# Full 128-column weights for the low halves of the probabilities, and scores issued last in a step, in an image attention kernel

## The chip, the cores and the metric

The kernel runs on one core of one Trainium2 chip. The metric is the time of one execution on the device in microseconds (us), lower is better. The core has a matrix engine (TensorE, PE in the profile, its weight loads PEld), a vector engine (VectorE, DVE), an activation engine (ScalarE, ACT), a third elementwise engine (GpSimd, POOL), and SyncE (SP), which starts most transfers. Each engine runs its own list of instructions in order; they wait for one another by semaphores alone.

## The reference

For each of 8 images x of 128 channels and 32 x 32 = 1024 positions:

```
g = x . w_g + b_g            (1024 x 64)
theta = x . w_theta + b_theta (1024 x 64);  phi = w_phi . x + b_phi (64 x 1024)
att = softmax(theta . phi)    (1024 x 1024, over the last axis)
y   = att . g                 (1024 x 64)
out = x + batch_norm(y . w_out + b_out)
```

The batch norm has fixed mean and variance, so it is a scale and a shift for each channel. All in fp32.

## The kernel before

**Tiles and steps.** An image has MT = 8 tiles of 128 query rows, so there are 64 tiles. Everything is a software pipeline over tiles: in step k, PE works on tile k+1 (scores), tile k-2 (transposes) and the values of an earlier group. Below, "step j" is step k with j = k % 8, the position in an image. A part of four tiles is a half image (512 queries).

**One tile's way.** PE multiplies theta and phi into a tile of scores, 128 x 1024, in PSUM (line 601, four matmuls of 512 columns: a product of high and low parts). DVE takes the row maximum (496), ACT the exponential with its row sum (455), DVE the reciprocal of the sum (518), POOL scales the probabilities by it (316), PE transposes them in eight pieces of 128 x 128 (663), ACT writes the fp16 high half pt_hi (446) and DVE the fp16 low half pt_lo (566), each in two instructions of 512 columns.

**Values.** `weighted_sum` sums y over the eight groups of 128 keys. g is split into two fp16 parts that lie beside each other in the 128 weight columns: columns 0 to 63 high, 64 to 127 low. In each step one quarter (two groups of keys) of a half image is added, to all 512 queries: two matmuls of the high halves with all 128 columns (616), two of the low halves with the 64 high columns alone (620). Of these two, one writes PSUM partitions 0 to 63 and the other 64 to 127, so they use the two column halves of the array ("column tiles"). The output weights stand twice one above the other, so the convolution (628) adds both halves of the partitions.

**Extras.** The next image is prepared in the same steps through one PSUM bank, ps_misc: its projections in steps 0 and 1 (687, three matmuls each), the output convolution of a finished half in steps 2 and 6 (628), g in step 3 (702), its transposition in step 4 (709), and the spread of g's largest value over the partitions after the values of step 7 (607). As all of them use ps_misc, each waits until its last user has been read: the projection of step 0 waits for g_peak_read, which DVE gives after reading the spread maximum in its own step 0 (535), and g in step 3 waits for result_ready, which DVE gives after adding the convolution to the residual in its own step 3 (501). Both waits stand for images 1 to 6; image 0 has neither, and image 7, having no next image, has no such extras.

**Order on DVE.** DVE's step k is written as: reciprocal of tile k-1, residual (j = 3, 7), largest value of g (j = 6) or its reading (j = 0), pt_lo of tile k-2 (twice), and last the row maximum of tile k+1. So the row maximum of tile k+1 stands in front of everything of step k+1.

**Order on ACT and POOL.** ACT's step k: extras, pt_hi of tile k-2 twice, exponential of tile k. POOL's step k: scaling of tile k-1, then extras. The images are run by a loop of two images for each turn, with steps before and after it written out.

Of the kernel before, what the change touches and what calls it, by code (L numbers as in the profile page):

```python
# [23 lines left out]
def build_nonlocal_attention(nc, x, w_tp_t, w_g_t, w_out_t, channel_vectors, out):  # L24
# [14 lines left out]
    CI = w_g_t.shape[1]  # L39
# [7 lines left out]
    MT = N // P  # L47
    TILES = B * MT
# [16 lines left out]
    with ExitStack() as ctx:  # L65
        def sbuf(name, shape, dt):
            return ctx.enter_context(nc.sbuf_tensor(name, shape, dt))
# [48 lines left out]
        pt_lo = [sbuf(f"pt_lo{i}", [P, MT, BANK], F16) for i in range(2)]  # L116
# [69 lines left out]
        def tile_at(it, k):  # L186
            return it * STEPS + k

        def half_at(it, k):
            return it * (STEPS // HALF_TILES) + k // HALF_TILES  # L190

        def image_at(it, k):
            return it * (STEPS // MT) + k // MT

        def exists(index, count):
            return not isinstance(index, int) or 0 <= index < count

        def wait(eng, semaphore, value):

            if not isinstance(value, int) or value > 0:  # L200
                eng.wait_ge(semaphore, value)
# [4 lines left out]
        def is_first(image):  # L206
            return isinstance(image, int) and image == 0
# [373 lines left out]
        def _(pe):  # L581
# [7 lines left out]
            def scores(t, it, k):  # L589


                r, cols = k // MT % 2, slice(k % MT * P, (k % MT + 1) * P)
                if k % MT == 0 and not (isinstance(t, int) and t == 0):
                    pe.wait_ge(stacked[r], it * 16 * STACKS + 16 * STACKS * ((k // MT + 1) // 2))
                if isinstance(t, int) and t < 2:
                    pe.wait_ge(first_lo, (NEEDED_BY_TILE_0, len(first_order))[t])
                wait(pe, probs_ready, t - 1)
                for n, phi in enumerate((phi_hh[r], phi_ll[r])):
                    for c in range(PER_IMAGE):
                        cc = slice(c * BANK, (c + 1) * BANK)  # L600
                        last = nc.tensor.matmul(ps_scores[k % 2][:, cc], theta_hl[r][:, cols], phi[:, cc],  # L601
                                                start=(n == 0), stop=(n == 1))
                last.then_inc(scores_ready, 1)
# [6 lines left out]
            def weighted_sum(quarters, ring, r, target, to, cols):  # L610


                g = g_parts[r]
                for quarter in quarters:
                    for m in (2 * quarter, 2 * quarter + 1):
                        nc.tensor.matmul(target[:, to], g[:, m, :], pt_hi[ring][:, m, cols],  # L616
                                         start=(m == 0), stop=False, skip_group_check=True)
                    for side in range(2):
                        m = 2 * quarter + side
                        last = nc.tensor.matmul(target[side * CI:(side + 1) * CI, to], g[:, m, 0:CI],  # L620
                                                pt_lo[ring][:, m, cols], start=False, stop=(m >= MT - 2),
                                                skip_group_check=True)
                if quarters[-1] == HALF_TILES - 1:
                    last.then_inc(y_ready, 1)

# [12 lines left out]
            for is_phi, cols, projected in first_order:  # L638
# [9 lines left out]
                             start=True, stop=True).then_inc(g_bias_ready, 1)  # L648
            pe.wait_ge(ident_ready, 1)

            def step(it, k):
                image, j = image_at(it, k), k % MT

                t = tile_at(it, k - 2)
                if exists(t, TILES):
                    pe.wait_ge(probs_scaled, t + 1)
                    for c in range(2):
                        if isinstance(t, int) and t == 0:
                            pe.wait_ge(*((g_out, 1), (shift_ready, 1))[c])
                        wait(pe, pt_lo_ready, 2 * t + c - 1)  # L660
                        for a in range(HALF_TILES):
                            m = c * HALF_TILES + a
                            last = nc.tensor.transpose(ps_flip[c][:, a * P:(a + 1) * P],  # L663
                                                       probs[(k - 2) % PROB_RING][:, m * P:(m + 1) * P],
                                                       ident[:, :])
                        last.then_inc(flipped, 1)

                t = tile_at(it, k + 1)
                if exists(t, TILES):
                    scores(t, it, k + 1)  # L670


                image, j = image_at(it, k), k % MT
                more = exists(image + 1, B)
                if j in (0, 1) and more:
                    if j == 0:

                        if isinstance(image, int) and image == 0:
                            pe.wait_ge(w_lo_ready, 1)
                        pe.wait_ge(x_lo_ready, 2 * image + 2)  # L680
                        if not is_first(image):
                            pe.wait_ge(g_peak_read, image + 1)
                    else:
                        pe.wait_ge(proj_out, 2 * image + 1)
                    cols = slice(j * BANK, (j + 1) * BANK)
                    for n, (w, xs) in enumerate(((w_tp_hi, x_hi), (w_tp_lo, x_hi), (w_tp_hi, x_lo))):
                        last = nc.tensor.matmul(ps_misc[:, :], w[:, :], xs[:, cols],  # L687
                                                start=(n == 0), stop=(n == 2))
                    last.then_inc(proj_ready, 1)
                h = half_at(it, k - 10)  # L690
                if j % HALF_TILES == 2 and exists(h, HALVES - 2):
                    if more:
                        pe.wait_ge(*((proj_out, 2 * image + 2) if j == 2 else (g_out, image + 2)))
                    else:
                        wait(pe, result_ready, h)
                    convolve(h, ps_misc[:, :], slice(0, BANK))

                if j == 3 and more:
                    wait(pe, proj_out, 2 * image + 2)
                    wait(pe, result_ready, 2 * image - 1)  # L700
                    for c in range(PER_IMAGE):
                        last = nc.tensor.matmul(ps_misc[c * CI:(c + 1) * CI, :], wg[:, :],  # L702
                                                x_in[(k // MT + 1) % 2][:, c * BANK:(c + 1) * BANK],
                                                start=True, stop=True, skip_group_check=True)
                    last.then_inc(g_ready, 1)
                if j == 4 and more:
                    pe.wait_ge(g_channels_out, image + 1)
                    for a in range(HALF_TILES):
                        last = nc.tensor.transpose(ps_misc[:, a * P:(a + 1) * P],  # L709
                                                   g_channels[:, a * P:(a + 1) * P], ident[:, :])  # L710
                    last.then_inc(g_flipped, 1)


                h, quarter = half_at(it, k - 6), (k - 6) % HALF_TILES
                if exists(h, HALVES - 2):
                    if quarter == 0:
                        pe.wait_ge(pt_lo_ready, 2 * HALF_TILES * h + 2 * HALF_TILES)
                        pe.wait_ge(g_split, image_at(it, k - 6) + 1)
                        wait(pe, y_scaled, h)
                    weighted_sum((quarter,), (k - 6) // HALF_TILES % 2, (k - 6) // MT % 2,  # L720
                                 ps_y, slice(0, BANK), slice(0, BANK))

                if tile_is(it, k, 1):
                    spread_peak(0, 0, ps_y[:, 0:P])
                if j == 7 and more:
                    wait(pe, result_ready, 2 * image)
                    spread_peak(image + 1, (k // MT + 1) % 2, ps_misc[:, 0:P])

                if tile_is(it, k, TILES - 2):
                    pe.wait_ge(pt_lo_ready, 2 * (TILES - HALF_TILES))  # L730
                    pe.wait_ge(g_split, B)
                    pe.wait_ge(y_scaled, HALVES - 2)
                for tile, quarters in ((TILES - 2, (0,)), (TILES - 1, (1, 2)), (TILES, (3,))):
                    if tile_is(it, k, tile):
                        weighted_sum(quarters, 0, 1, ps_y, slice(0, BANK), slice(0, BANK))
# [44 lines left out]
```

## Time and profile before

| | us |
|---|---|
| median of three runs | 232.55 (231.91 to 232.59) |
| profiled execution, its own time | 232.21 |
| its span, first to last instruction | 230.4 |
| PE busy | 223.3 |
| DVE busy | 184.2 |
| ACT busy | 171.1 |
| POOL busy | 148.9 |

The span is the part of an execution that the trace covers; 1.8 us lie around it. A busy PE means that some matmul was in flight, so its start-to-start distances say more than its durations. The granted TensorE clock is 1.00 throughout, the upper of its two levels (2.4 GHz).

### The profile page before, as it was taken

To read this page: it belongs to the slowest core of one execution; us is meant where nothing else is said; L and a number is where in the kernel's file an instruction comes from. 1 tells how busy PE (TensorE), PEld (TensorE's weight loads), DVE (VectorE), ACT (ScalarE), POOL (GpSimd) and SP (SyncE) were. 2 spreads that over 40 slices of the span, in tenths; PEclk is the share of its full clock that TensorE was granted. 3 is DMA by queue.
4 is the path that set the end of the run, shared out by engine and by line. 5 is a ranking of instruction groups with operands and counts; after the bars stand their busy time and mean duration, and the time that the engine had idled before them with its cause. 6 is when DMAs were issued, how large, how long until landed. Compare 5 with 4: busy or idle time off the path is not lost.

```text
span 230.4 us, 4277 instructions
## 1 busy us (share of the span) xinstructions
PE 223.3 (97%) x1228; PEld 141.4 (61%) x1228; DVE 184.2 (80%) x328; ACT 171.1 (74%) x311; POOL 148.9 (65%) x143
## 2 busy tenths in 40 slices
PE   7997899999999999999999999999999999999994
PEld 6684756655674667566666656746575566656542
DVE  0789997779968798868987699687988689989751
ACT  2687968778786877779687778859777896868641
POOL 2557888757785777775797578856777733934400
PEclk9999999999999999999999999999999999999999
DMA  5107320654108510365106441084101651010111
GB/s 172 51 0 213 88 65 3 174 123 115 46 7 222 152 47 34 101 172 137 46 0 185 119 106 48 22 246 120 67 3 23 159 137 46 0 46 0 48 45 46
DMA packets 8716, 19.78 MB, mean 86 GB/s; under 512 B 1536, under 2 KB 2048, under 8 KB 8704
## 3 DMA queue, kind: packets, MB, share of 16 engines
q1 hardware_dynamic: 8416, 19.50, 30.8%
q10 hardware_dynamic: 288, 0.14, 0.2%
q8 instruction: 5, 0.08, 0.2%
q14 instruction: 7, 0.06, 0.1%
HBM read 4.43 MB, written 4.19 MB: 37 GB/s over the span
## 4 chain that ended last, share of the span: by engine, by line
PE 88%; DVE 5%; DMA 3%; POOL 1%; SPq 0%; issue 0%; ACT 0%; DVEq 0%
PE ps_flip L663 25%; PE ps_scores L601 24%; PE ps_y L616 12%; PE ps_y L620 9%; PE ps_misc L628 6%; PE ps_misc L687 4%; PE ps_misc L702 3%; DVE neg_max L496 2%; DMA phi_ll<-lo 2%; PE ps_scores L640 2%; DMA w_tp<-w_tp_t_dram 2%; DVE pt_lo L566 1%; PE ps_misc L607 1%; PE ps_misc L709 1%; PE ps_flip L585 1%; DVE g_parts L550 1%
## 5 line engine op out<-in xcount | busy, mean ns | idle before, releaser
L316 POOL TENSOR_SCALAR probs<-probs,inv_sum 128x1024 f32<-128x1024 f32 x64 | 72.3, 1129 | 63.5 <-DVE inv_sum L518 63.0
L566 DVE SCALAR_TENSOR_TENSOR pt_lo<-ps_flip,pt_hi 128x512 f16<-128x512 f32 x128 | 82.3, 685 | 31.5 <-ACT pt_hi L446 31.3
L446 ACT ACTIVATE pt_hi<-ps_flip 128x512 f16<-128x512 f32 x128 | 69.5, 594 | 42.6 <-PE ps_flip L663 42.5
L496 DVE TENSOR_REDUCE neg_max<-ps_scores 128x1 f32<-128x1024 f32 x64 | 77.8, 1215 | 0.7 <-PE ps_scores L601 0.6
L663 PE MATMUL ps_flip<-ident,probs 128*128 128x128 f32 x512 | 69.7, 279 | 2.3 <-DVE pt_lo L566 1.5
L455 ACT ACTIVATE probs<-ps_scores,neg_max 128x1024 f32<-128x1024 f32 x64 | 71.5, 1118 | 0.0
L663 PEld LDWEIGHTS ps_flip<-ident,probs 128*128 128x128 f32 x512 | 55.2, 141 | 16.5 <-issue 10.0
L601 PE MATMUL ps_scores<-phi_hh,theta_hl 128*128 128x512 f32 x128 | 45.5, 436 | 0.3 <-DMA phi_ll<-lo 0.3
L601 PE MATMUL ps_scores<-phi_ll,theta_hl 128*128 128x512 f32 x128 | 40.0, 393 | 0.0
L616 PE MATMUL ps_y<-pt_hi,g_parts 128*128 128x512 f16 (+1 forms) x128 | 38.1, 379 | 0.0
L601 PEld LDWEIGHTS ps_scores<-phi_ll,theta_hl 128*128 128x128 f32 x128 | 24.0, 188 | 5.7
L620 PE MATMUL ps_y<-pt_lo,g_parts 128*64 128x512 f16 (+1 forms) x128 | 25.8, 400 | 0.0
L620 PEld LDWEIGHTS ps_y<-pt_lo,g_parts 128*64 128x64 f16 x128 | 7.0, 106 | 26.7 <-issue 26.7
L616 PEld LDWEIGHTS ps_y<-pt_hi,g_parts 128*128 128x128 f16 x128 | 9.2, 98 | 22.7 <-issue 19.3
L601 PEld LDWEIGHTS ps_scores<-phi_hh,theta_hl 128*128 128x128 f32 x128 | 19.4, 191 | 0.6 <-DMA phi_ll<-lo 0.5
L342 POOL TENSOR_TENSOR lo<-qk,hi 128x512 fp32r<-128x512 f32 x14 | 18.0, 1285 | 0.0
L371 POOL TENSOR_TENSOR x_lo<-x_in,x_hi 128x512 fp32r<-128x512 f32 x14 | 17.8, 1273 | 0.1
L628 PE MATMUL ps_misc<-y_norm,wout 128*128 128x512 f32 x30 | 15.3, 593 | 0.0
L394 ACT ACTIVATE y_norm<-ps_y,y_unit 128x512 f32<-128x512 f32 (+1 forms) x16 | 10.9, 682 | 3.9 <-PE ps_y L620 3.1
L455 ACT ACTIVATION_READ_ACCUMULATOR probs<-ps_scores,neg_max 128x1 f32 x64 | 13.5, 212 | 0.0
L501 DVE SCALAR_TENSOR_TENSOR resid<-ps_misc,bn,resid 128x512 f32<-128x512 f32 x15 | 11.0, 733 | 0.0
L518 DVE RECIPROCAL inv_sum<-row_sum 128x1 f32<-128x1 f32 x64 | 9.8, 153 | 0.3 <-ACT probs L455 0.3
(77 smaller groups left out, 162.0 us busy)
## 6 DMA issues: line engine op xcount, KB each, us to landing
x_in<-x_in_dram SPq DMA_DIRECT2D x16, 256.0 KB, 3.2
out_dram<-resid SPq DMA_DIRECT2D x15, 256.0 KB, 2.0
phi_hh<-hi SPq DMA_DIRECT2D x14, 256.0 KB, 4.4
phi_ll<-lo SPq DMA_DIRECT2D x14, 256.0 KB, 4.0
theta_hl<-hi SPq DMA_DIRECT2D x7, 256.0 KB, 3.4
theta_hl<-lo SPq DMA_DIRECT2D x7, 256.0 KB, 3.1
out_dram<-resid SPq DMA_DIRECT2D x1, 192.0 KB, 2.1
w_tp<-w_tp_t_dram ACTq DMA_DIRECT2D x1, 128.0 KB, 3.5
```

Source lines behind the costliest of these rows:

```text
L316: nc.gpsimd.tensor_scalar(out=p[:, :], in0=p[:, :], scalar1=inv_sum[:, at:at + 1], scalar2=1.0, op0=ALU.mult, op1=ALU.mult).then_inc(probs ...
L342: nc.gpsimd.tensor_tensor(lo[:, cols], qk[:, cols], hi[:, cols].bitcast(F32), ALU.subtract).then_inc(lo_ready, 1)
L371: nc.gpsimd.tensor_tensor(x_lo[:, cols], x_in[r][:, cols], x_hi[:, cols].bitcast(F32), ALU.subtract).then_inc(x_lo_ready, 1)
L446: nc.scalar.activation(pt_hi[ring][:, c * HALF_TILES:(c + 1) * HALF_TILES, slot * P:(slot + 1) * P], ps_flip[c][:, :].rearrange("p (a n) - ...
L455: nc.scalar.activation(probs[k % PROB_RING][:, :], ps_scores[k % 2][:, :], ACT.Exp, bias=neg_max[:, k % STEPS:k % STEPS + 1], accum_out=ro ...
L496: nc.vector.tensor_reduce(out=neg_max[:, k % STEPS:k % STEPS + 1], in_=ps_scores[k % 2][:, :], op=ALU.max, axis=AX.X, negate=True).then_in ...
L566: nc.vector.scalar_tensor_tensor(out=pt_lo[ring][where], in0=ps_flip[c][:, :].rearrange("p (a n) -> p a n", n=P), scalar=PROB_SCALE, in1=p ...
L601: last = nc.tensor.matmul(ps_scores[k % 2][:, cc], theta_hl[r][:, cols], phi[:, cc], start=(n == 0), stop=(n == 1))
L616: nc.tensor.matmul(target[:, to], g[:, m, :], pt_hi[ring][:, m, cols], start=(m == 0), stop=False, skip_group_check=True)
L620: last = nc.tensor.matmul(target[side * CI:(side + 1) * CI, to], g[:, m, 0:CI], pt_lo[ring][:, m, cols], start=False, stop=(m >= MT - 2), ...
L628: nc.tensor.matmul(target, wout[:, 0:C], y_norm[:, cols], start=True, stop=True).then_inc(conv_ready, 1)
L663: last = nc.tensor.transpose(ps_flip[c][:, a * P:(a + 1) * P], probs[(k - 2) % PROB_RING][:, m * P:(m + 1) * P], ident[:, :])
```

## The change

In `weighted_sum` the two matmuls of the low halves take all 128 weight columns of g and write all 128 PSUM partitions, one after the other, as the high halves do. Each now also adds the product of g's low part with the low half of the probabilities. In PE's step the scores of tile k+1 are issued after the values instead of right after the transposes; the extras stay ahead of the values.

```diff
@@ weighted_sum
-                    for side in range(2):
-                        m = 2 * quarter + side
-                        last = nc.tensor.matmul(target[side * CI:(side + 1) * CI, to], g[:, m, 0:CI],
-                                                pt_lo[ring][:, m, cols], start=False, stop=(m >= MT - 2),
-                                                skip_group_check=True)
+                    for m in (2 * quarter, 2 * quarter + 1):
+                        last = nc.tensor.matmul(target[:, to], g[:, m, :], pt_lo[ring][:, m, cols],
+                                                start=False, stop=(m == MT - 1), skip_group_check=True)
@@ PE's step, after the transposes
-                t = tile_at(it, k + 1)
-                if exists(t, TILES):
-                    scores(t, it, k + 1)
@@ PE's step, after weighted_sum and before spread_peak
+                t = tile_at(it, k + 1)
+                if exists(t, TILES):
+                    scores(t, it, k + 1)
```

Two lines fall away in all, so some lines after 618 have smaller numbers in the changed kernel: 620 is 619 there, 628 is 626, 663 is 661, 687 is 681, 702 is 696, 709 is 703.

On PE, step 3 of an image in the loop read as follows before; ps_flip are the transposes, ps_misc<-x_in is g of the next image, ps_y are the values.

```order
L663 MATMUL ps_flip<-ident,probs 128x128 [waits pt_lo_ready]
L663 MATMUL ps_flip<-ident,probs 128x128 x3
L201 REGISTER_ALU
L601 MATMUL ps_scores<-phi_hh,theta_hl 128x512 [waits probs_ready]
L601 MATMUL ps_scores<-phi_hh,theta_hl 128x512
L601 MATMUL ps_scores<-phi_ll,theta_hl 128x512 x2
L201 REGISTER_ALU [waits proj_out]
L702 MATMUL ps_misc<-x_in,wg 64x512 [waits result_ready]
L702 MATMUL ps_misc<-x_in,wg 64x512
L616 MATMUL ps_y<-pt_hi,g_parts 128x512 x2
L620 MATMUL ps_y<-pt_lo,g_parts 64x512 x2
```

After the change, the same place:

```order
L661 MATMUL ps_flip<-ident,probs 128x128 [waits pt_lo_ready]
L661 MATMUL ps_flip<-ident,probs 128x128 x3
L201 REGISTER_ALU [waits proj_out]
L696 MATMUL ps_misc<-x_in,wg 64x512 [waits result_ready]
L696 MATMUL ps_misc<-x_in,wg 64x512
L616 MATMUL ps_y<-pt_hi,g_parts 128x512 x2
L619 MATMUL ps_y<-pt_lo,g_parts 128x512 x2
L201 REGISTER_ALU
L601 MATMUL ps_scores<-phi_hh,theta_hl 128x512 [waits probs_ready]
L601 MATMUL ps_scores<-phi_hh,theta_hl 128x512
L601 MATMUL ps_scores<-phi_ll,theta_hl 128x512 x2
```

The four score matmuls have moved from between the transposes and g to behind the values, and g with its wait for result_ready follows the transposes directly.

On PE, step 0 of an image in the loop, from behind the transposes on, before; ps_misc<-x_hi are the projections:

```order
L601 MATMUL ps_scores<-phi_hh,theta_hl 128x512 [waits probs_ready]
L601 MATMUL ps_scores<-phi_hh,theta_hl 128x512
L601 MATMUL ps_scores<-phi_ll,theta_hl 128x512 x2
L680 ISA
L682 REGISTER_ALU [waits x_lo_ready]
L687 MATMUL ps_misc<-x_hi,w_tp_hi 128x512 [waits g_peak_read]
L687 MATMUL ps_misc<-x_hi,w_tp_lo 128x512
L687 MATMUL ps_misc<-x_lo,w_tp_hi 128x512
L616 MATMUL ps_y<-pt_hi,g_parts 128x512 x2
L620 MATMUL ps_y<-pt_lo,g_parts 64x512 x2
```

After the change:

```order
L674 ISA
L676 REGISTER_ALU [waits x_lo_ready]
L681 MATMUL ps_misc<-x_hi,w_tp_hi 128x512 [waits g_peak_read]
L681 MATMUL ps_misc<-x_hi,w_tp_lo 128x512
L681 MATMUL ps_misc<-x_lo,w_tp_hi 128x512
L616 MATMUL ps_y<-pt_hi,g_parts 128x512 x2
L619 MATMUL ps_y<-pt_lo,g_parts 128x512 x2
L201 REGISTER_ALU
L601 MATMUL ps_scores<-phi_hh,theta_hl 128x512 [waits probs_ready]
L601 MATMUL ps_scores<-phi_hh,theta_hl 128x512
L601 MATMUL ps_scores<-phi_ll,theta_hl 128x512 x2
```

The projection, with its waits for x_lo_ready and g_peak_read, now comes ahead of the scores. The instructions of DVE, ACT, POOL and SP and their order are the same in both kernels.

## Rows read from the trace of the kernel before

**Rows 1.** The page: PE's busy time in the span, and the other engines'

```profile
PE 223.3 (97%) x1228; PEld 141.4 (61%) x1228; DVE 184.2 (80%) x328; ACT 171.1 (74%) x311; POOL 148.9 (65%) x143
```

**Rows 2.** Stretches of an image: length, then busy time of PE, PEld, DVE, ACT, POOL

```profile
90.47:117.24 26.77, 26.77 (x150) 16.87 (x148) 22.17 (x40) 20.80 (x39) 19.55 (x18) 1.00 0.36 98
```

**Rows 3.** Waits, 40 to 196 us: waiting engine and line, total us, times, longest

```profile
PEld ps_y L620 <- issue: 19.9, 47, 0.4
```

**Rows 4.** Groups of instructions: line 616, count, then busy us, mean ns of one

```profile
L616 PE MATMUL ps_y<-pt_hi,g_parts 128*128 128x512 f16 (+1 forms) x128 | 38.1, 379 | 0.0
```

**Rows 5.** Timeline of PE, a step 5: start us, length us, what it is

```profile
131.26 1.09 PE L663 MATMUL ps_flip<-ident,probs 128*128 128x128 f32 x8
132.11 0.71 PE L601 MATMUL ps_scores<-phi_hh,theta_hl 128*128 128x512 f32 x2
132.66 0.62 PE L601 MATMUL ps_scores<-phi_ll,theta_hl 128*128 128x512 f32 x2
133.12 0.60 PE L616 MATMUL ps_y<-pt_hi,g_parts 128*128 128x512 f16 x2
133.66 0.41 PE L620 MATMUL ps_y<-pt_lo,g_parts 128*64 128x512 f16 x2
133.99 1.10 PE L663 MATMUL ps_flip<-ident,probs 128*128 128x128 f32 x8
```

**Rows 6.** Timeline of PE: ends of steps 7 and 3, extras of steps 0, 3

```profile
113.54 0.49 PE L607 MATMUL ps_misc<-ident,g_peak 128*128 128x128 f32 x2
113.87 1.04 PE L663 MATMUL ps_flip<-ident,probs 128*128 128x128 f32 x8
...
115.67 0.39 PE L687 MATMUL ps_misc<-x_hi,w_tp_hi 128*128 128x512 f32 x1
...
116.38 0.60 PE L616 MATMUL ps_y<-pt_hi,g_parts 128*128 128x512 f16 x2
...
124.27 1.09 PE L663 MATMUL ps_flip<-ident,probs 128*128 128x128 f32 x8
...
126.22 1.08 PE L702 MATMUL ps_misc<-x_in,wg 128*64 128x512 f32 x4
127.23 0.60 PE L616 MATMUL ps_y<-pt_hi,g_parts 128*128 128x512 f16 x2
```

**Rows 7.** Timeline of DVE: reading in step 0, then row maximum to row maximum, step 3

```profile
114.53 0.27 DVE L535 TENSOR_REDUCE g_peak_all<-ps_misc 128x1 f32<-128x128 f32 x1
...
123.22 1.22 DVE L496 TENSOR_REDUCE neg_max<-ps_scores 128x1 f32<-128x1024 f32 x1
124.35 0.15 DVE L518 RECIPROCAL inv_sum<-row_sum 128x1 f32<-128x1 f32 x1
124.42 0.73 DVE L501 SCALAR_TENSOR_TENSOR resid<-ps_misc,bn,resid 128x512 f32<-128x512 f32 x1
125.59 1.29 DVE L566 SCALAR_TENSOR_TENSOR pt_lo<-ps_flip,pt_hi 128x512 f16<-128x512 f32 x2 [0.44 <-ACT pt_hi L446]
126.80 1.22 DVE L496 TENSOR_REDUCE neg_max<-ps_scores 128x1 f32<-128x1024 f32 x1
```

**Rows 8.** Timeline of ACT, step 3

```profile
124.96 1.08 ACT L446 ACTIVATE pt_hi<-ps_flip 128x512 f16<-128x512 f32 x2 [1.40 <-PE ps_flip L663]
125.93 1.12 ACT L455 ACTIVATE probs<-ps_scores,neg_max 128x1024 f32<-128x1024 f32 x1
```

**Rows 9.** Timeline of POOL, step 1: the scaling

```profile
117.80 1.12 POOL L316 TENSOR_SCALAR probs<-probs,inv_sum 128x1024 f32<-128x1024 f32 x1 [0.56 <-DVE inv_sum L518]
```

**Rows 10.** Timeline of PE, start of the program: scores of tile 1

```profile
12.38 0.62 PE L601 MATMUL ps_scores<-phi_ll,theta_hl 128*128 128x512 f32 x2
```

**Rows 11.** Timeline of DVE, start of the program: row maximum of tile 1

```profile
13.04 1.22 DVE L496 TENSOR_REDUCE neg_max<-ps_scores 128x1 f32<-128x1024 f32 x1 [0.60 <-PE ps_scores L601]
```

**Rows 12.** Timeline of PE, end of the program: transposes with values right behind them

```profile
214.97 1.09 PE L663 MATMUL ps_flip<-ident,probs 128*128 128x128 f32 x8
215.89 0.59 PE L616 MATMUL ps_y<-pt_hi,g_parts 128*128 128x512 f16 x2
```

## The prediction

> **What bounds the kernel now.** I read the page first, then the stretches of an image, the waits, and the timelines of PE, DVE, ACT and POOL over one image. PE is busy 223.3 of a span of 230.4 us, the next engine 184.2 [rows 1], and in an image in the middle it has a matmul in flight for all of 26.77 us [rows 2]. So PE sets the time, nothing else is waited for there, and a wait that the change puts on PE is paid in full.
>
> Start-to-start distances give PE's own price of a plain step (step 5, no extras) [rows 5]: transposes 0.85 (131.26 to 132.11), scores 1.01 (to 133.12), high halves 0.54 (to 133.66), low halves 0.33 (to 133.99), together 2.73 us. The extras add 0.71 for a projection and 1.01 for g [rows 6].
>
> **The low halves.** The two 64-column matmuls last 0.41 together though each streams 512 columns, and the next instruction starts 0.33 after them [rows 5]: they run side by side. What do they cost beyond one stream? One full matmul of 512 columns takes 0.22 to 0.23 from start to start (0.46 for two of line 601; the two of line 616 last 0.60 together and one of them 0.38 [rows 4, 5]). So the high pair should hand over after 0.44 and does so after 0.54, about 0.10 lost on the way into the column tiles: the weight load of line 620 sits idle 0.4 us before each of 47 pairs, as no other in the step does [rows 3, 5]. On the way out 0.33 instead of 0.22 is another 0.11, and the transposes behind it last 1.09 for eight against 1.04 behind line 607, another 0.05 [rows 5, 6]. The block thus costs 0.87 + 0.05 = 0.92 now. Four full matmuls cost 4 x 0.22 = 0.88, if nothing else is lost; bounds 0.84 (the pair of 0.59 [rows 12] less 0.38, so 0.21 each) and 0.92 (0.23 each, as line 601). The row that shows transposes and full values in sequence gives 0.92 for eight transposes behind column tiles [rows 12], so 0.86 without the 0.05; the way from fp16 values to scores stands in no row, between 0 and the 0.10 of the column switch. I take -0.05 us a step, bounds -0.08 (0.84) and +0.10 (0.92 and the switch). The PE price of a step becomes 0.87 + 0.88 + 0.93 = 2.68.
>
> The Trainium skill (TensorEngine Tiling, Key Properties) says that tiles run in parallel, and that changing the tiling mode drains TensorE. By its first half alone the low halves would double in stream, 0.22 us x 62 steps = 13.6 us more; its second half is what the 0.10 and 0.11 look like. By the rows the one about pays for the other.
>
> **The order: what comes late.** Let 0 be the start of the transposes of a step. Scores of the tile whose row maximum opens DVE's list for step j now end with PE's step j-1. Four score matmuls end 1.17 after their start (132.11 to 133.28 [rows 5]), 1.08 without the slower first one behind transposes, and DVE starts 0.04 after that (13.00 and 13.04 [rows 10, 11]). PE has issued them in 0.93, so the row maximum starts at about 0.2 of the next step (1.12 less 0.93). Before it started at 123.22 for the step beginning at 124.27, 1.05 ahead. DVE's next items follow by its own rows [rows 7]: row maximum 1.13 to the next start, reciprocal 0.07, residual 0.73 long (0.65 to the next start, estimated from its length less the usual overlap), pt_lo pair 1.21. So reciprocal at 1.3, then:
>
> - **Step 3, images 1 to 6.** Residual from 1.4 to 2.13, g on PE from 2.17. g would otherwise start at 0.87. Before, the residual ran from 0.15 to 0.88 of its step, g came at 1.95 (124.42 and 126.22 less 124.27) [rows 6, 7], so the wait had 1.07 to spare. New step: 2.17 + 1.01 + 0.88 + 0.93 = 4.99 against 3.83 (124.27 to g's start 1.95, g 1.01, values 0.87): **+1.16**.
> - **Step 0, images 1 to 6.** Step 7 has a residual too, so DVE's pt_lo pair ends only at 1.4 + 0.65 + 1.21 = 3.25 of step 7, which now takes PE 2.68 + 0.33 = 3.01; the row maximum starts at 0.24 of step 0, the reciprocal at 1.37, the reading of the spread maximum (0.27 long [rows 7]) ends at 1.71, and the projection starts at 1.76 instead of 0.87. New step 1.76 + 0.71 + 0.88 + 0.93 = 4.28 against 3.38 (113.87 to the values at 116.38, and 0.87 for them [rows 6]): **+0.90**.
> - **Step 5, and steps without extras in image 7.** POOL starts its scaling 1.43 after the row maximum starts (the reciprocal starts at +1.13; its length of 0.15 and as much again for the hand-over is my estimate of the 0.3 more), takes 1.12 [rows 9], PE may go 0.05 later: 0.2 + 2.6 = 2.80 at least from one step to the next where the step before was not held, against 2.73: **+0.07**.
> - **Steps 1, 2, 4, 6, 7**: -0.05 each, **-0.25**. The convolution in step 2 waits for y_norm, behind qk on ACT: ACT has pt_hi from 0.69 and the exponential from 1.66 of step 1 (124.96 and 125.93 less 124.27 [rows 6, 8]), is free at 2.76, then come qk and y_norm, 512 columns each as pt_hi, so estimated at 0.6 each with a little for the last one's end: 4.1. As the step is 3.39 long, that is 0.7 of step 2. PE wants it at 0.87. Hidden, with 0.2 to spare. Only an exponential more than 0.2 late would show.
>
> That is 1.9 us for each image. From step 1 of image 1 to the end of image 6 it comes 6 times, less one step 0 (counted at the start): 11.3 - 0.9 = **10.5**.
>
> **Start.** The second pair of tile 1's scores starts at 12.38, and DVE has sat idle for 0.6 when they end, so PE's order sets the pace there; DVE's own chain follows from that row maximum on [rows 10, 11]. A projection of 0.71 now goes ahead of them, another ahead of tile 2's. Bounds 0.7 and 1.4 us; through DVE's chain I take **+1.0** up to step 1 of image 1, the first step 0 with a wait included. **End.** Image 7 has no waits for ps_misc's readers, but DVE's step 0 and its residual in step 3 fall in steps of 2.7 to 2.8 us where its own list is 3.1 long (1.20 + 0.65 + 1.21), so the row maximum slips 0.3 to 0.4 and with it the scaling: **+0.7**. The values behind the last steps run without transposes: -0.05 for each of the eight last quarters, **-0.4**.
>
> **The sum** is 10.5 + 1.0 + 0.7 - 0.4 = 11.8 us on the profiled execution's own 232.21. The median of the runs stands 0.34 above that, so 244.4 us (244.35).
>
> **Rivals.**
> 1. *As above, both waits pay* (0.74): by the bounds on values (-0.03 to +0.15 a step around my value, of which a third over 60 steps is -0.6 to +3 us), on the start, and 0.1 for refilling PE after each of 12 waits, 241.5 to 248.5.
> 2. *More chains close* (0.09): with the scores last, the round of row maximum, reciprocal, scaling, transposes has 0 to 0.2 us to spare in most steps. If each link costs 0.1 more than in my walk, the 30 steps or so that are near it lose 0.1 to 0.2 each: 248 to 252. Against it: a step with a projection or a convolution has 0.6 to 0.7 to spare (3.4 and 3.5 against 2.80), and five of eight steps have one or are held anyway.
> 3. *The column switch isn't saved* (0.05): if the 0.10 and 0.11 belong to something else, such as changing between pt_hi and pt_lo, the low halves cost 0.22 more a step, 244.4 + 13.6 = 258 us. The one matmul more in each pair streams those 0.22 in 62 steps. Against it: g of step 3, which uses column tiles too, starts 0.10 later behind the same transposes and scores than values do (1.95 from 124.27 to 126.22, against 1.86 from 131.26 to 133.12 [rows 5, 6]). The Trainium skill's rule of parallel tiles, taken alone (TensorEngine Tiling, Key Properties), would give this time.
> 4. *Only one of the two waits shows* (0.07), because DVE gets to its residual or to the spread maximum sooner than my walk has it: 237 to 240.
> 5. *Faster* (0.03), and *no change* (0.02). The place is DVE in steps 3 and 0: if the row maximum that now opens its list started 1.2 us earlier than PE's order lets it, both readings would end before 0.87 and PE would keep the 0.05 of the blocks: 232.55 - 3 = 229.5. It decides at 0.87 us after the first transpose. Against it: DVE's list is fixed and its first item needs the last item of PE's step before.
>
> **Numbers.** The likeliest is 244.4. Cases 1 and the nearer parts of 2 and 4 hold 8 in 10 within 240.5 to 249.5. Differences under 0.3% (0.7 us) count as none for this kernel's measurement: faster 0.03, within 0.02, slower 0.95.
>
> **What would show it.** In the changed kernel's timeline of PE: a gap of about 1.3 us before g in step 3, released by DVE's residual, in six images, and of 0.9 before the projection in step 0, released by the reading of the spread maximum; row maxima on DVE starting 0.2 after the transposes; DVE's idle time before pt_lo, mostly gone; four ps_y matmuls 0.22 apart and the next engine item 0.88 behind the first; plain steps of 2.7 to 2.8. A middle image should take 28.7 us instead of 26.77. The prediction is wrong if that image stays under 27.5 (waits hidden), or if the four value matmuls take over 1 us.

## The result, and the profile after

The changed kernel takes 244.74 us (median of four runs, 244.3 to 246.87) against 232.23 us for the kernel before in the same comparison (four runs, 231.9 to 232.59). The ratio is 1.056, 95% interval 1.0515 to 1.0606: slower by 5.6%. The forecast was 244.4 us.

The page of the changed kernel, its engines' busy times:

```profile
PE 223.7 (92%) x1228; PEld 155.0 (64%) x1228; DVE 184.4 (76%) x328; ACT 171.8 (71%) x311; POOL 148.9 (61%) x143
```

PE's work is what it was (223.3 before [rows 1]), in a span that grew from 230.4 to 242.6 us. So PE now waits in the middle of the program, where it had a matmul in flight all the time before [rows 2]. Who it waits for stands in the waits of the whole span (waiting engine and line, what releases it, total us, times, longest):

```profile
DVE neg_max L496 <- PE ps_scores L601: 43.1, 49, 1.9
...
PE ps_misc L696 <- DVE resid L501: 7.0, 6, 1.2
...
PE ps_misc L681 <- DVE g_peak_all L535: 4.3, 6, 0.8
...
PEld ps_misc L681 <- POOL x_lo L371: 3.1, 3, 1.0
```

The two waits forecast are there, six times each: g of step 3 (696) on the residual (501), 7.0 us by the matmuls, and the projection of step 0 (681) on the reading of the spread maximum (535), 4.3 us. On the other side DVE now sits idle 43 us ahead of the row maximum, waiting for scores, where it had waited 31 us for pt_hi before. The row for x_lo is the weight load of the same projection in three of the six images. It stands for the same wait: in the image shown below x_lo ended at 120.97 and the reading at 121.67, so the reading ended last.

Two images in the middle, stretches from the transposes of a step 0 to those of the next (length, then busy PE, PEld, DVE, ACT, POOL):

```profile
119.87:148.84 28.97, 26.91 (x151) 18.63 (x149) 22.24 (x40) 20.96 (x38) 19.56 (x19) 1.00 0.33 91
148.84:177.80 28.96, 26.98 (x150) 18.75 (x150) 22.30 (x40) 20.92 (x38) 19.62 (x19) 1.00 0.33 91
```

28.97 us an image against 26.77 [rows 2], and PE is without a matmul in flight for 2.1 of them.

PE's timeline, step 0, the start of step 1, and step 3 of the first of the two, then the start of step 0 of the second:

```profile
119.87 1.12 PE L661 MATMUL ps_flip<-ident,probs 128*128 128x128 f32 x8
121.81 0.47 PE L681 MATMUL ps_misc<-x_hi,w_tp_hi 128*128 128x512 f32 x1 [0.82 <-DVE g_peak_all L535]
...
124.38 1.03 PE L661 MATMUL ps_flip<-ident,probs 128*128 128x128 f32 x8
...
131.28 1.04 PE L661 MATMUL ps_flip<-ident,probs 128*128 128x128 f32 x8
133.48 1.08 PE L696 MATMUL ps_misc<-x_in,wg 128*64 128x512 f32 x4 [1.16 <-DVE resid L501]
134.49 0.60 PE L616 MATMUL ps_y<-pt_hi,g_parts 128*128 128x512 f16 x2
134.94 0.59 PE L619 MATMUL ps_y<-pt_lo,g_parts 128*128 128x512 f16 x2
135.18 0.82 PE L601 MATMUL ps_scores<-phi_hh,theta_hl 128*128 128x512 f32 x2
135.84 0.63 PE L601 MATMUL ps_scores<-phi_ll,theta_hl 128*128 128x512 f32 x2
136.31 0.93 PE L661 MATMUL ps_flip<-ident,probs 128*128 128x128 f32 x7
...
148.84 1.10 PE L661 MATMUL ps_flip<-ident,probs 128*128 128x128 f32 x8
150.67 0.50 PE L681 MATMUL ps_misc<-x_hi,w_tp_hi 128*128 128x512 f32 x1 [0.73 <-DVE g_peak_all L535]
```

In step 0 eight transposes start at 119.87 and the projection at 121.81, 1.94 later (forecast 1.76); in the next image it is 1.83. Images 2 to 6 take turns so, 1.94 to 1.99 in one and 1.83 or 1.85 in the next. In step 3 g starts 2.20 after the transposes (forecast 2.17), where it had started at 1.95 with the scores in between [rows 6]. The step with g lasts 131.28 to 136.31, 5.03 us against 4.99 forecast. The value block shows the other half of the change: the second pair (619) starts 0.45 after the first (616) and the scores 0.24 behind the second. The first pair of scores now takes 0.66 to the start of the next pair, where it took 0.55 [rows 5].

DVE's timeline at the same two places:

```profile
120.19 1.21 DVE L496 TENSOR_REDUCE neg_max<-ps_scores 128x1 f32<-128x1024 f32 x1
...
121.40 0.27 DVE L535 TENSOR_REDUCE g_peak_all<-ps_misc 128x1 f32<-128x128 f32 x1
...
131.48 1.23 DVE L496 TENSOR_REDUCE neg_max<-ps_scores 128x1 f32<-128x1024 f32 x1 [1.05 <-PE ps_scores L601]
132.62 0.15 DVE L518 RECIPROCAL inv_sum<-row_sum 128x1 f32<-128x1 f32 x1
132.69 0.73 DVE L501 SCALAR_TENSOR_TENSOR resid<-ps_misc,bn,resid 128x512 f32<-128x512 f32 x1
```

In step 3 the row maximum starts at 131.48, 0.20 after the transposes of 131.28, having waited 1.05 us for scores (it had started 1.05 ahead of its step [rows 6, 7]). The reciprocal follows after 1.14, the residual at 132.69, and its end at 133.42 releases g at 133.48. Nothing in this list got slower; it starts later.

### The profile page after: what moved, and what is told of

Read it like the earlier page. It is cut to its first block, busy times and chain, and to the rows that moved or that the text cites. A ratio compares the mean times of both kernels' runs of the same rounds, so it can differ in the third digit from the quotient of the medians.

```text
span 242.6 us, 4276 instructions
## 1 busy us (share of the span) xinstructions
PE 223.7 (92%) x1228; PEld 155.0 (64%) x1228; DVE 184.4 (76%) x328; ACT 171.8 (71%) x311; POOL 148.9 (61%) x143
## 4 chain that ended last, share of the span: by engine, by line
PE 75%; DVE 12%; issue 7%; DMA 1%; POOL 1%; ACT 1%; DVEq 1%; POOLq 0%
PE ps_scores L601 21%; PE ps_flip L661 17%; PE ps_y L616 10%; PE ps_y L619 10%; PE ps_misc L626 5%; PE ps_misc L681 4%; DVE pt_lo L566 4%; DVE neg_max L496 3%; PE ps_misc L696 3%; DVE resid L501 3%; DMA w_tp<-w_tp_t_dram 1%; PE ps_scores L638 1%; PE ps_misc L703 1%; DVE inv_sum L518 1%; POOL probs L316 1%
## 5 line engine op out<-in xcount | busy, mean ns | idle before, releaser
L661 PE MATMUL ps_flip<-ident,probs 128*128 128x128 f32 x512 | 68.1, 276 | 2.7 <-DVE pt_lo L566 1.3
L661 PEld LDWEIGHTS ps_flip<-ident,probs 128*128 128x128 f32 x512 | 57.8, 141 | 16.4 <-POOL probs L316 6.7
L601 PE MATMUL ps_scores<-phi_hh,theta_hl 128*128 128x512 f32 x128 | 51.3, 481 | 0.0
L619 PE MATMUL ps_y<-pt_lo,g_parts 128*128 128x512 f16 (+1 forms) x128 | 37.6, 376 | 0.0
L601 PEld LDWEIGHTS ps_scores<-phi_hh,theta_hl 128*128 128x128 f32 x128 | 23.9, 190 | 9.7 <-issue 1.3
L616 PEld LDWEIGHTS ps_y<-pt_hi,g_parts 128*128 128x128 f16 x128 | 11.0, 98 | 17.3 <-issue 16.1
L619 PEld LDWEIGHTS ps_y<-pt_lo,g_parts 128*128 128x128 f16 x128 | 12.5, 98 | 14.7
L696 PE MATMUL ps_misc<-x_in,wg 128*64 128x512 f32 x28 | 7.6, 618 | 7.0 <-DVE resid L501 7.0
```

Of the source, the lines that this page charges most:

```text
L619: last = nc.tensor.matmul(target[:, to], g[:, m, :], pt_lo[ring][:, m, cols], start=False, stop=(m == MT - 1), skip_group_check=True)
```

## The experiments

Times are medians; ratios are against the kernel before in the same comparison. The differences between kernels of this section are taken between their medians. The median of the kernel before lay between 231.90 and 232.23 us in the comparisons that they come from, and the four runs of the changed kernel spread from 244.3 to 246.87, so a difference against the changed kernel is good to some 0.5 us.

### Only the order

```diff
 changed kernel, weighted_sum
-                    for m in (2 * quarter, 2 * quarter + 1):
-                        last = nc.tensor.matmul(target[:, to], g[:, m, :], pt_lo[ring][:, m, cols],
-                                                start=False, stop=(m == MT - 1), skip_group_check=True)
+                    for side in range(2):
+                        m = 2 * quarter + side
+                        last = nc.tensor.matmul(target[side * CI:(side + 1) * CI, to], g[:, m, 0:CI],
+                                                pt_lo[ring][:, m, cols], start=False, stop=(m >= MT - 2),
+                                                skip_group_check=True)
```

> The changed kernel with the 64-column low halves put back, so only the order of the step is changed. Theory (two waits in steps 3 and 0 carry the loss, the two forms of the low halves cost PE about the same): each step is 0.05 us dearer than in the changed kernel, but that delay also shortens nothing else, so 244.7 + 1.5 to 3 = 246 to 248 us, and both waits stand as they do. Rival (the full weights cost 0.22 us more a step and the order costs nothing): about 232 us.

Measured: 249.64 us, ratio 1.076 (1.0736 to 1.0779). The order alone costs 17.6 us, and the full weights give 4.9 of it back; the expectation had 1.5 to 3, and 246 to 248 us in all. Both waits stand as in the changed kernel, six times each.

### Only the weights

```diff
 kernel before, weighted_sum
-                    for side in range(2):
-                        m = 2 * quarter + side
-                        last = nc.tensor.matmul(target[side * CI:(side + 1) * CI, to], g[:, m, 0:CI],
-                                                pt_lo[ring][:, m, cols], start=False, stop=(m >= MT - 2),
-                                                skip_group_check=True)
+                    for m in (2 * quarter, 2 * quarter + 1):
+                        last = nc.tensor.matmul(target[:, to], g[:, m, :], pt_lo[ring][:, m, cols],
+                                                start=False, stop=(m == MT - 1), skip_group_check=True)
```

> The kernel before with full weights for the low halves, scores where they were. Theory: 60 steps at -0.05 us, less up to 0.1 us where the scores follow elsewhere: 229 to 231 us. Rival (the column switch isn't saved, the second stream of 0.22 us is paid in 62 steps): about 246 us.

Measured: 227.83 us, ratio 0.981 (0.9792 to 0.9825). This half of the change alone is faster than both kernels, by 4.2 us against the one before; that is 1.2 us below the expected range. Its step 5 on PE's timeline:

```profile
129.55 1.04 PE L661 MATMUL ps_flip<-ident,probs 128*128 128x128 f32 x8
130.35 0.71 PE L601 MATMUL ps_scores<-phi_hh,theta_hl 128*128 128x512 f32 x2
130.90 0.62 PE L601 MATMUL ps_scores<-phi_ll,theta_hl 128*128 128x512 f32 x2
131.36 0.61 PE L616 MATMUL ps_y<-pt_hi,g_parts 128*128 128x512 f16 x2
131.81 0.59 PE L619 MATMUL ps_y<-pt_lo,g_parts 128*128 128x512 f16 x2
132.24 0.93 PE L661 MATMUL ps_flip<-ident,probs 128*128 128x128 f32 x7
```

Transposes 0.80, scores 1.01, high pair 0.45, low pair 0.43: 2.69 us in all, against 2.73 [rows 5]. The low pair costs 0.43 instead of 0.33, but the way into it has lost its 0.09 and the transposes behind it their 0.05 (1.04 long, as behind line 607 [rows 6]). The whole image takes 26.27 us against 26.77, 0.06 for each of eight steps. Another 0.94 us come from the last step of the program, where the values are summed in pieces of 384 and 128 columns: 5.35 us from its transposes to the last convolution, against 6.29.

### g behind the scores, and the projection behind the scores

```diff
 changed kernel, PE's step: the block of step 3 (g) moved
-                if j == 3 and more:
...
                 t = tile_at(it, k + 1)
                 if exists(t, TILES):
                     scores(t, it, k + 1)
 
+                if j == 3 and more:
...
```

> The changed kernel with g of step 3 behind the scores, where DVE's residual is long done. Theory: the six waits of 1.2 to 1.3 us go, so 244.7 - 7.3 = 237.4 us, with up to 0.5 us back because the transposes of g in step 4 now wait for their evacuation: 237 to 238.5. Rival (the wait only stands where another would, such as DVE's or POOL's round): over 242 us.

Measured: 237.46 us, ratio 1.0229 (1.0211 to 1.0247), 7.3 us less than the changed kernel, as expected. The waits on the residual are gone; those on the reading of the spread maximum stand (4.4 us, six times).

```diff
 changed kernel, PE's step: the projection of step 0 moved, that of step 1 left
-                if j in (0, 1) and more:
...
+                def project():
+                    if j in (0, 1) and more:
...
+                if j == 1:
+                    project()
...
                 if exists(t, TILES):
                     scores(t, it, k + 1)
+
+                if j == 0:
+                    project()
```

> The changed kernel with the projection of step 0 behind the scores, in every image. Theory: the six waits of 0.9 to 1.1 us go (one of them partly at the start), and tile 1's scores no longer stand behind a projection at the start, -0.5: 244.7 - 6.0 - 0.5 = 238.2, less what step 1's projection then waits for ACT's qk (0.1 us in each of seven images): 238 to 239.5. Rival (another wait takes its place): over 242 us.

Measured: 239.96 us, ratio 1.0343 (1.0323 to 1.0364), 4.8 less than the changed kernel, 0.5 short of the expected range. On its timeline step 0 shrinks from 4.51 to 3.46 us, but step 1 grows from 3.38 to 3.56: its projection now starts 0.94 after the transposes, not 0.79, and 0.05 after ACT's qk has ended (122.16). That wait had been foreseen with 0.1 us; step 1 grows by 0.15 to 0.18 in the six images:

```profile
117.81 1.13 PE L661 MATMUL ps_flip<-ident,probs 128*128 128x128 f32 x8
...
121.27 1.04 PE L661 MATMUL ps_flip<-ident,probs 128*128 128x128 f32 x8
122.21 0.50 PE L682 MATMUL ps_misc<-x_hi,w_tp_hi 128*128 128x512 f32 x1
...
124.83 1.03 PE L661 MATMUL ps_flip<-ident,probs 128*128 128x128 f32 x8
```

By the traces the six steps 0 of images 1 to 6 lose 5.9 us, near the 6.0 expected, and their steps 1 give 0.96 back. The expected gain of 0.5 at the start did not come: step 1 of image 0 waits 0.78 us for qk there, and step 0 of image 1 begins at 33.80 instead of 33.55. So this wait is worth 5.9 us, of which moving the projection gives 4.8. Each of the two moves was made alone; no run has both.

### The same waits taken away on DVE

In these PE's scores stay last. First the residual goes ahead of the row maximum, one step earlier in DVE's list:

```diff
 changed kernel, DVE's step
-                h = half_at(it, k - 11)
-                if j % HALF_TILES == 3 and exists(h, HALVES - 2):
-                    ring, part = (k - 11) // MT % 2, (k - 11) // HALF_TILES % PER_IMAGE
-                    dve.wait_ge(resid_ready, image_at(it, k - 11) + 1)
-                    add_residual(h, resid[ring][:, part * BANK:(part + 1) * BANK], ps_misc[:, :])
...
+                h = half_at(it, k - 10)
+                if j % HALF_TILES == 2 and exists(h, HALVES - 2):
+                    ring, part = (k - 10) // MT % 2, (k - 10) // HALF_TILES % PER_IMAGE
+                    dve.wait_ge(resid_ready, image_at(it, k - 10) + 1)
+                    add_residual(h, resid[ring][:, part * BANK:(part + 1) * BANK], ps_misc[:, :])
                 t = tile_at(it, k + 1)
                 if exists(t, TILES):
                     row_maximum(t, k + 1)
```

> The changed kernel with PE's order untouched; on DVE the residual is added at the end of steps 2 and 6, ahead of the row maximum, instead of in steps 3 and 7 behind it. Theory (the wait of step 3 stands only because the residual is queued behind a row maximum that waits for the scores): its 1.3 us go six times, and step 7's DVE list gets 0.65 shorter, so the row maximum ahead of step 0's reading starts 0.4 to 0.45 earlier, six times; 0.3 more in image 7: 244.7 - 7.8 - 2.5 - 0.3 = 234.1 us, range 233 to 236. Rival (PE's order itself costs the time, through longer rounds that DVE's order can't shorten): over 240 us.

Measured: 234.47 us, ratio 1.0105 (1.0089 to 1.012): 10.3 us less without moving one PE instruction, and inside the expected range. Step 3 shrinks from 5.03 to 3.78 us and step 0 from 4.51 to 4.16. The rival, over 240 us because PE's order itself costs the time, is out; that the order costs something besides the two waits shows in the next run. DVE's timeline of step 2 and the row maximum of step 3 shows that the residual fits in the idle time ahead of the row maximum, which still waits 0.39 us for scores:

```profile
124.88 1.27 DVE L561 SCALAR_TENSOR_TENSOR pt_lo<-ps_flip,pt_hi 128x512 f16<-128x512 f32 x2
126.06 0.74 DVE L501 SCALAR_TENSOR_TENSOR resid<-ps_misc,bn,resid 128x512 f32<-128x512 f32 x1
127.19 1.22 DVE L496 TENSOR_REDUCE neg_max<-ps_scores 128x1 f32<-128x1024 f32 x1 [0.39 <-PE ps_scores L601]
```

Then the spread maximum too, ahead of the scores on PE in step 7 and read ahead of the row maximum on DVE:

```diff
 on top of that, PE's step: ahead of the scores instead of behind them
+                if j == 7 and more:
+                    wait(pe, result_ready, 2 * image)
+                    spread_peak(image + 1, (k // MT + 1) % 2, ps_misc[:, 0:P])
                 t = tile_at(it, k + 1)
 and DVE's step, ahead of row_maximum (image 0 keeps its own in step 2)
+                if j == 7 and exists(image + 1, B):
+                    r = (k // MT + 1) % 2
+                    dve.wait_ge(g_peak_spread, image + 2)
...
```

> As the kernel with the residual first, and in step 7 the spread maximum is issued ahead of the scores on PE and read on DVE ahead of the row maximum. Theory: the rest of step 0's wait, about 0.6 us, goes six times: about 230.5 us. Against the kernel with full weights and the scores early (227.8) there remain the start (1.0), the 0.25 of each image's step 5, and the slips in image 7, 0.5 to 1 us. Rival (the scores last cost more than the two waits): 232 us or more.

Measured: 232.59 us, ratio 1.003 (1.0019 to 1.004). The expectation of 230.5 missed by 2.1, and the value lies in the rival's range. The order does cost more than the two waits. Its waits between 40 and 196 us, those of PE:

```profile
PEld ps_flip L678 <- DVE pt_lo L561: 4.5, 11, 0.5
...
PEld ps_misc L698 <- POOL x_lo L371: 0.9, 3, 0.3
...
PEld ps_flip L678 <- POOL probs L316: 0.2, 1, 0.2
```

The two waits are gone, but transposes wait, by this list for pt_lo, and the projection of step 0 waits for POOL's x_lo. On PE's timeline, steps 0 and 5 (their transposes, what follows, and the next transposes):

```profile
114.17 1.09 PE L678 MATMUL ps_flip<-ident,probs 128*128 128x128 f32 x8
115.33 0.50 PE L698 MATMUL ps_misc<-x_hi,w_tp_hi 128*128 128x512 f32 x1
...
117.91 1.04 PE L678 MATMUL ps_flip<-ident,probs 128*128 128x128 f32 x8
118.70 0.48 PE L698 MATMUL ps_misc<-x_hi,w_tp_hi 128*128 128x512 f32 x1
...
131.68 1.04 PE L678 MATMUL ps_flip<-ident,probs 128*128 128x128 f32 x8
...
134.60 1.09 PE L678 MATMUL ps_flip<-ident,probs 128*128 128x128 f32 x8
...
141.11 1.09 PE L678 MATMUL ps_flip<-ident,probs 128*128 128x128 f32 x8
```

In step 0 the projection starts 1.16 after the transposes instead of 0.79 as in step 1, so 0.37 more, held by x_lo, which on POOL's timeline ends at 115.28:

```profile
114.01 1.27 POOL L371 TENSOR_TENSOR x_lo<-x_in,x_hi 128x512 fp32r<-128x512 f32 x1
```

In the same image step 5 lasts 2.92 us against 2.69 with the scores early. This image takes 26.94 us (114.17 to 141.11) against 26.27. The whole kernel takes 4.8 us more than the full weights alone by the medians, and 4.4 by the two traces: 0.15 up to step 1 of image 1 (37.12 against 36.97), 3.42 in the five images from there, 0.19 in the rest of image 6, and 0.64 from image 7 on. The expectation had counted the 0.25 of step 5 and forgotten x_lo, which is 0.4 in each image; the 1.0 that it counted for the start does not show in this pair of traces.

### The first image with its scores early

```diff
 changed kernel, PE's step
+                if is_first(image) and exists(tile_at(it, k + 1), TILES):
+                    scores(tile_at(it, k + 1), it, k + 1)
                 more = exists(image + 1, B)
...
                 t = tile_at(it, k + 1)
-                if exists(t, TILES):
+                if exists(t, TILES) and not is_first(image):
                     scores(t, it, k + 1)
```

> The changed kernel, but in the first image (steps 0 to 7) the scores are issued right behind the transposes, as before the change. Theory (the start costs 1.0 us, through projections ahead of the scores of tiles 1 and 2): 243.6 to 244.0 us. Rival (the start is set by the loads and DVE's own list and gains nothing): 244.5 to 245.

Measured: 243.47 us, ratio 1.0498 (1.0484 to 1.0513), 1.3 less than the changed kernel's median and 0.8 less than its fastest run; the expected range ended 0.1 above. Step 1 of image 1 begins at 36.60 instead of 37.66. In the two other kernels with the scores early in the first image it begins at 36.93 (before) and 36.97 (full weights alone), so by the traces the start costs 0.7 to 1.1 us; 1.0 was forecast.

### What one low matmul costs in either form

Both kernels leave out half of the products of the low halves. In the kernel before, the second column tile's matmul is not issued (`for side in range(1)`):

> The kernel before without the second of the two 64-column matmuls of each quarter, so half of the low halves' products is left out. Theory (the two run side by side, and the 0.33 us of the pair is one stream and the switch): within 0.5 us of the kernel before, 231.5 to 232.5. Rival (they run one after the other): 0.15 us or more less in each of 62 quarters, 222 us or less.

Measured: 231.63 us, ratio 0.9981 (0.9971 to 0.9992). In the kernel with full weights alone, one of the two low matmuls is not issued (`for m in (2 * quarter + 1,)`):

> The kernel with full weights and the scores early, without the first of the two low matmuls of each quarter, so half of the low halves' products is left out. Theory (a full matmul streams for 0.22 us of its own): 0.22 x 60 = 13 us less where PE sets the time, less in the steps of 2.5 us in which DVE's 2.4 us come near: 215 to 220 us. Rival (the full matmul is as good as free behind the others): over 225 us.

Measured: 215.33 us, ratio 0.9284 (0.9258 to 0.9309), 12.5 us less than with both. Both lie in their expected ranges, and both rivals are out. A quarter's end on PE's timeline, first with one column tile, then with one full matmul:

```profile
133.22 0.60 PE L616 MATMUL ps_y<-pt_hi,g_parts 128*128 128x512 f16 x2
133.76 0.40 PE L620 MATMUL ps_y<-pt_lo,g_parts 128*64 128x512 f16 x1
134.09 0.33 PE L663 MATMUL ps_flip<-ident,probs 128*128 128x128 f32 x1
```

```profile
124.51 0.60 PE L616 MATMUL ps_y<-pt_hi,g_parts 128*128 128x512 f16 x2
124.95 0.38 PE L619 MATMUL ps_y<-pt_lo,g_parts 128*128 128x512 f16 x1
125.17 1.04 PE L661 MATMUL ps_flip<-ident,probs 128*128 128x128 f32 x8
```

One column tile alone (133.76) still holds up the next transposes for 0.33 us and enters 0.54 behind the high pair: the second tile costs nothing, and what the pair takes beyond one stream of 0.22 is there with one tile as well. One full matmul (124.95) hands over after 0.22.

## Why the prediction was right, and where a term was off

**The waits and their price.** The mechanism was right, and is shown from both sides: moving g or the projection behind the scores on PE gave back 7.3 and 4.8 us, and moving the residual ahead of the row maximum on DVE gave back 10.3 with PE's order untouched. In the trace step 3 takes 5.03 us for 4.99, step 0 4.51 for 4.28. Step 0 is the mis-sized part, for three reasons. Step 7 took 2.93 us instead of 3.01, as the matmuls of line 607 took 0.26 (119.61 to 119.87) where 0.33 was counted, so DVE's list, which is full there, was further behind (row maximum at 0.32, not 0.24). The projection started 0.14 after the reading's end (121.67 to 121.81) in three of the images, those that the list puts under x_lo; in the other three it was 0.05 or 0.06 (150.62 to 150.67), as forecast. Why it alternates is open. And the three matmuls of the projection took 0.78 (121.81 to 122.59), not 0.71. Five images from step 1 to step 1 cost 2.14 us each by the trace (37.66 to 182.23 now, 36.93 to 170.80 before, 10.7 in all) against 1.9.

The forecast's walk also left x_lo out. In the changed kernel it ends at 120.97, 1.10 after the transposes of 119.87, so it would hold the projection past its 0.79 even if the reading came early. The reading, which ends 0.7 later, hides this; with the reading moved forward it showed as some 0.4 us in each image.

**The low halves.** Right in kind: the 0.10 and 0.11 go with the column tiles, the forecast's -0.05 a step is -0.04 in step 5 and -0.06 over an image. The rival that the switch would not be saved is refuted by the weights alone (227.83, not 246). In the new order the gain is larger, 4.9 us, 0.08 a step: the scores' first pair behind full fp16 values takes 0.65, but it starts 0.24 after the low pair, so values and scores take 1.82 (134.49 to 136.31); with column tiles in the same order they took 1.91 (136.62 to 138.53). The Trainium skill (TensorEngine Tiling (Array Packing), Key Properties) states that tiles run in parallel and that a change of tiling mode drains TensorE. The traces agree with the first half, as the second column tile is free, and with a cost where the second half puts one, about 0.2 us each time round. The drain itself shows in no row, and no run separates it from a cost of the 64-column matmuls as such.

**Step 5 and image 7.** Step 5 took 2.92, not 2.80 (139.40 to 142.32), and image 7's steps 0 to 5 took 18.06 us (206.54 to 224.60) against 17.19 before (194.19 to 211.38), 0.87 for 0.7. Of what the transposes behind step 5 need, POOL's scaling ends last:

```profile
141.07 1.12 POOL L316 TENSOR_SCALAR probs<-probs,inv_sum 128x1024 f32<-128x1024 f32 x1 [0.73 <-DVE inv_sum L518]
```

It started 1.67 after the transposes of 139.40 (forecast 1.63) and ended at 142.19; the transposes came at 142.32, 0.13 later and not 0.05. The list of waits puts this one under pt_lo, but DVE's pt_lo pair had ended at 142.08. By these ends the chain was the forecast one, and its hand-over was mis-sized. No run changed POOL's part, so this is read and not tested, and why 0.13 passed is open: where the list names the scaling, the transposes followed it by 0.06 (27.79 to 27.85). The kernel with both waits removed shows the same 2.92.

**Start and end.** Step 1 of image 1 came 0.73 late in the profiled execution, 1.0 was forecast. From step 6 of image 7 to the end it was 1.0 us shorter (18.0 against 19.0), not 0.4: in the last four quarters of 128 columns the forecast's 0.05 was too small. There sixteen matmuls take 0.90 us (237.36 to 238.26) where they took 1.58.

**The sum.** By the two traces the terms are 0.7 up to step 1 of image 1 (forecast 1.0), 11.6 from there to the end of image 6 (10.5), 0.9 to step 6 of image 7 (0.7), and -1.0 from there on (-0.4): 12.2 us, where the forecast added up 11.8. The errors of the start and the end act against those of steps 0 and 5, so that 244.4 met 244.74 this closely is partly luck. Some slips of the working change little. Its 11.3 - 0.9 is 10.4 and not 10.5, and 0.92 less 0.05 is 0.87 and not 0.86 (the sum uses 0.87). The low pairs with 512 columns are 60 and not 62, which puts the third rival at 257.6 and not 258 us. The second rival's 30 steps at 0.1 to 0.2 make 247.4 to 250.4 us, not 248 to 252.

## What to carry to other kernels

When the first item in an engine's list for a step waits for a late producer, everything queued behind it is late too: when a producer's output is moved to the end of a step, look at what its consumer has queued behind it, and who waits for that. Here the largest single cure with the scores kept last was on the consumer's side, the residual moved ahead of the wait into idle time (10.3 us); no kernel with the scores last came down to the 227.83 us of the one that leaves them early. Two half-width matmuls side by side were not cheaper here than two full ones, 0.92 us for the value block against 0.88: count what is lost on the way in and out against the stream that they save. And a change of two parts should be timed in parts, since here one half (-4.2 us) was hidden by the other (+17.6).

## What the runs showed of the hardware

Entering column tiles behind full-width matmuls cost 0.09 to 0.10 us and leaving them 0.11, plus 0.05 on transposes behind them, and the number of tiles did not matter: with one tile used the same 0.33 us passed. Not expected was that scores directly behind full fp16 values are recorded as starting only 0.24 after the low pair's start, with 0.65 or 0.66 for their first pair instead of 0.55: the sum, 1.82 us for values and scores, is that of the plain streams (0.88 + 0.93), so here a single recorded start on PE did not price the hand-over, only a longer stretch did. Transposes behind full fp16 values pay nothing (eight in 1.04 us, as behind line 607). In the changed kernel TensorE's granted clock reads 1.00 over the span, its upper level (2.4 GHz), through twelve waits of 0.4 to 1.2 us.
